# A decoder layer with experts: the router run by itself for the last two pairs, and new step orders and bank homes

## What is computed

```python
x = layernorm(x + attn(x, x, x, sa_..., causal=True))            # 16 heads of width 8
x = layernorm(x + attn(x, ctx, ctx, ca_..., causal=False))
rw = softmax(x @ router_w + router_b); topw, topi = top_k(rw, 2); topw = softmax(topw)
h = gelu(einsum('td,edf->etf', x, w1) + b1); eo = einsum('etf,efd->etd', h, w2) + b2
x = layernorm(x + sum over the two chosen experts of topw * eo)
```

## Time and profile before

| what | value |
|---|---|
| time, median of 3 runs | 417.77 us (416.07 to 417.9) |
| time of the profiled execution | 417.14 us |
| its span, first to last instruction | 415.4 us |
| busy: PE, PEld, DVE, ACT, POOL | 323.3, 240.7, 247.2, 224.1, 182.5 us |
| mean granted clock of PE | 0.889 of 2.4 GHz |

### The profile page before, as it was taken

How to read it: one execution, slowest core, us unless ns; L and a number is a source line. 1 busy time by engine, 2 the same in 40 slices (tenths; PEclk the granted TensorE clock), 3 DMA queues, 4 the chain that set the end, 5 groups by cost and what they waited for, 6 DMA issues and landing times. The chain is left out here.

```text
span 415.4 us, 8711 instructions
## 1 busy us (share of the span) xinstructions
PE 323.3 (78%) x2242; PEld 240.7 (58%) x2242; DVE 247.2 (60%) x793; ACT 224.1 (54%) x560; POOL 182.5 (44%) x260
## 2 busy tenths in 40 slices
PE   2589899998999889988798745886885779999400
PEld 1445576866767646655556422774684668999400
DVE  7062847585687772796564675254276554666356
ACT  4227385857867655666555512548653424556224
POOL 8404343451553583534834527002246556455422
PEclk9979999999999996999989965599798688999855
DMA  7453242344453532441437762322701123220053
GB/s 196 110 167 73 63 100 62 85 102 136 100 157 71 135 131 54 88 153 40 132 85 212 236 176 87 69 55 77 201 9 34 34 70 92 64 54 30 11 197 101
DMA packets 35047, 42.09 MB, mean 101 GB/s; under 512 B 5819, under 2 KB 26160, under 8 KB 35001
## 3 DMA queue, kind: packets, MB, share of 16 engines
q1 hardware_dynamic: 32728, 37.31, 33.8%
q0 software_dynamic: 2272, 4.24, 3.2%
HBM read 13.66 MB, written 14.79 MB: 68 GB/s over the span
## 5 line engine op out<-in xcount | busy, mean ns | idle before, releaser
L1426 POOL DMA_INDIRECT results<-sa_us,sa_pt x39 | 39.9, 1023 | 69.5 <-DVE sa_us L1326 65.7
L1056 ACT ACTIVATE sa_us<-bank,expert_b 128x128 f32<-128x128 f32 x156 | 44.7, 370 | 36.9 <-PE bank L905 36.3
L1391 POOL TENSOR_SCALAR_AFFINE_SELECT sa_pt<-sa_pt 128x512 f32<-128x512 f32 x64 | 38.7, 636 | 56.5 <-ACT sa_pt L1002 56.5
L1129 DVE TENSOR_REDUCE sa_nm<-bank 128x4 f32<-128x512 f32 x64 | 41.4, 685 | 20.9 <-PE bank L791 20.7
L918 PE MATMUL bank<-sa_over_qm,sa_us 128*128 x312 | 46.7, 298 | 8.4 <-ACT sa_us L1056 3.8
L918 PEld LDWEIGHTS bank<-sa_over_qm,sa_us 128*128 128x128 f32 x312 | 41.8, 208 | 11.8 <-issue 11.8
L905 PE MATMUL bank<-xsT,sa_pt 128*128 128x128 f32 x312 | 47.5, 301 | 1.3 <-DVE sa_pt L1314 1.0
L1002 ACT ACTIVATE ca_pt<-bank 77x512 f32<-77x512 f32 x64 | 34.4, 588 | 20.8 <-PE bank L811 20.8
L905 PEld LDWEIGHTS bank<-xsT,sa_pt 128*128 128x128 f32 x312 | 42.9, 212 | 3.3 <-DVE xsT L1313 1.5
L1421 POOL DMA_INDIRECT dispatched<-r_sent,r_row x32 | 31.1, 973 | 28.6 <-issue 17.1
L1129 DVE TENSOR_REDUCE ca_nm<-bank 128x4 f32<-128x308 f32 x64 | 27.6, 474 | 22.2 <-PE bank L791 21.8
(11 more groups left out here) (213 smaller groups left out, 752.2 us busy)
## 6 DMA issues: line engine op xcount, KB each, us to landing
dispatched<-filler SPq DMA_DIRECT2D x17, 520.0 KB, 4.7
sa_km<-sa_ku SPq DMA_DIRECT2D x32, 128.0 KB, 2.4
sa_qm<-sa_qu SPq DMA_DIRECT2D x32, 96.0 KB
ca_qm<-ca_qu SPq DMA_DIRECT2D x32, 96.0 KB
sa_pt<-dispatched SPq DMA_DIRECT2D x39, 65.0 KB, 1.8
ca_km<-ca_ku SPq DMA_DIRECT2D x32, 77.0 KB, 2.1
sa_over_km<-in_e_w SPq DMA_DIRECT2D x1, 2048.0 KB, 12.6
sa_pt<-results SPq DMA_DIRECT2D x8, 256.0 KB, 5.8
```

Source lines behind the costliest of these rows:

```text
L1056: act.activation(hid[n % 2][:, c, :], bank[b][:, P * (c if n < EARLY else c % 2):][:, 0:P], ACT.Gelu, bias=b1[:, bass.ds(expert * FC + c, ...
L1129: dve.tensor_reduce(k.nm[:, u, :, g], bank[home_of(p)[k, "scores", u][g % 2]][:, :].rearrange("q (j n) -> q j n", j=J)[:, :, 0:k.keys], AX ...
L1391: pool.affine_select(out=blockg, in_=blockg, compare_op=ALU.is_ge, fill=0.0, base=0, pattern=[[0, J], [1, P]], channel_multiplier=-1).then ...
L1426: pool.indirect_dma_start(out=results, out_offset=bass.IndirectOffsetOnAxis(ap=xs[n % RING][:, P:P + 1].bitcast(I32), axis=0), in_=ys[n % ...
```

## The change

For pairs 0 to 5 the router works as before. For pairs 6 and 7 it runs once for each pair, on that pair's two token tiles: 31 DVE operations instead of 33 (one running sum in place of three), each on half the columns; two exponentials on ACT for each pair; PE's `place` for each; and four transfers of POOL for each instead of eight for both. `routed_at` and `router_run` hold the counts that the waits use.

The fill of `dispatched` counts on two semaphores instead of one, so POOL waits for two values where it waited for one; the semaphore `s_fill` is gone and the filler counts on `s_pool_ones`.

All tables of `ORDER`, `FINAL`, `home` and `last_home` are new: the same steps in another order on each engine and in other banks.

```diff
-        ROUTER_OPS = 33
-        SELECTED = 20
+        ALONE = PAIRS - 2
+        def routed_at(p):
+            if p < ALONE:
+                return p % 2 == 1, slice(0, 4), p // 2 * 33, p // 2 * 33 + 20, p // 2 * 33 + 33
+            n = ALONE // 2 * 33 + (p - ALONE) * 31
+            return True, slice(2 * (p % 2), 2 * (p % 2) + 2), n, n + 18, n + 31
+        def router_run(p):
+            return p // 2 if p < ALONE else ALONE // 2 + p - ALONE
...
-                if p % 2 == 0:
+                runs, w, before, selected, after = routed_at(p)
+                if not runs:
                     return
...
-                pe.wait_ge(r.s_rt, n * ROUTER_OPS + SELECTED)
+                pe.wait_ge(r.s_rt, selected)
...
-                pool.wait_ge(s_filled, p * 32 + 32)
-                pool.wait_ge(r.s_rt, (p // 2 + 1) * ROUTER_OPS)
+                for n in range(p - (w.stop - w.start) // 2 + 1, p + 1):
+                    pool.wait_ge(s_filled[n % 2], n // 2 * 32 + 32)
+                pool.wait_ge(r.s_rt, after)
                 pool.wait_ge(r.s_xe1, p + 1)
-                for v in range(4):
+                for v in range(w.start, w.stop):
...
-            (CA, "mix", 0): (2,), (CA, "mix", 1): (5,), (CA, "norm", 0): (1,), (CA, "norm", 1): (4,),
+            (CA, "mix", 0): (1,), (CA, "mix", 1): (4,), (CA, "norm", 0): (1,), (CA, "norm", 1): (5,),
...
-            (CA, "weights", 1): (0, 3), (RT, "place", 0): (1,), (RT, "route", 0): (2, 2), (SA, "mix", 0): (2,),
+            (CA, "weights", 1): (7, 2), (RT, "place", 0): (4,), (RT, "route", 0): (2, 4), (SA, "mix", 0): (7,),
```

More of the change, by code:

```diff
@@ L306, in build @@
-            "pe": [
[L307 to L320, removed]
@@ new lines, in build @@
+                (CA, "weights", 1, 4), (RT, "gate", 0, 4), (SA, "project", 0, 7), (SA, "project_keys", 0, 7),
+                (MOE, "bias_columns", 0, 0), (SA, "turn_heads", 1, 5), (RT, "route", 0, 3), (SA, "shift", 0, 6),
+                (RT, "gate", 0, 3), (CA, "weights", 2, 4), (CA, "mix", 0, 4), (CA, "weights", 3, 4),
+                (SA, "weights", 0, 6), (SA, "weights", 1, 6), (CA, "turn", 0, 5), (RT, "second", 0, 3),
+                (SA, "shift", 1, 6), (CA, "spread_keys", 0, 5), (CA, "turn_context", 0, 6), (CA, "spread_keys", 1, 5),
@@ L484, in build @@
-                (CA, "project", 0, 6), (SA, "values", 0, 7), (CA, "norm", 1, 5), (SA, "restore", 0, 7),
-                (CA, "scores", 0, 6), (RT, "gate", 0, 5), (CA, "scores", 1, 6), (RT, "choose", 0, 5), (CA, "shift", 0, 6),
-                (RT, "second", 0, 5), (SA, "restore", 1, 7), (RT, "place", 0, 4), (RT, "place", 0, 5),
-                (RT, "number", 0, 5), (CA, "scores", 2, 6), (SA, "norm", 0, 7), (CA, "scores", 3, 6),
-                (CA, "project_keys", 0, 7), (CA, "shift", 1, 6), (MOE, "table", 0, 0), (RT, "second", 0, 6),
@@ L533, in build @@
-            (SA, "turn", 0): (2,), (SA, "turn_heads", 0): (3,), (SA, "turn_heads", 1): (6,), (SA, "values", 0): (0,),
-            (SA, "weights", 0): (4, 7), (SA, "weights", 1): (5, 6)}
+            (CA, "mix", 0): (4,), (CA, "mix", 1): (2,), (CA, "norm", 0): (4,), (CA, "project", 0): (1,),
+            (CA, "project_keys", 0): (5,), (CA, "restore", 1): (4,), (CA, "scores", 0): (5, 4), (CA, "scores", 1): (4, 5),
+            (CA, "shift", 0): (1,), (CA, "shift", 1): (5,), (CA, "spread_keys", 0): (0,), (CA, "spread_keys", 1): (3,),
@@ new lines, in build @@
+            (CA, "spread_terms", 1): (1,), (CA, "turn", 0): (4,), (CA, "turn_context", 0): (1,),
+            (CA, "turn_heads", 0): (5,), (CA, "turn_heads", 1): (5,), (CA, "values", 0): (5,), (CA, "weights", 0): (1, 2),
+            (CA, "weights", 1): (7, 5), (RT, "place", 0): (5,), (RT, "route", 0): (0, 7), (SA, "mix", 0): (1,),
+            (SA, "mix", 1): (0,), (SA, "norm", 0): (0,), (SA, "norm", 1): (4,), (SA, "project", 0): (1,),
+            (SA, "project_keys", 0): (0,), (SA, "restore", 1): (2,), (SA, "scores", 0): (4, 5), (SA, "scores", 1): (1, 6),
@@ L536, in home_of @@
+            (SA, "shift", 0): (0,), (SA, "shift", 1): (7,), (SA, "spread_terms", 0): (6,), (SA, "spread_terms", 1): (7,),
+            (SA, "turn", 0): (4,), (SA, "turn_heads", 0): (4,), (SA, "turn_heads", 1): (1,), (SA, "values", 0): (5,),
+            (SA, "weights", 0): (7, 0), (SA, "weights", 1): (3, 5)}
         def home_of(p):
@@ L1257, in _ @@
+                assert done[0] == after, done[0]
             tables = [0]
```

521 lines of the change are left out of this document (264 added, 257 removed).

## The result

The changed kernel takes 394.21 us (median of 4 runs, 391.07 to 396.04) against 416.92 for the kernel before on the same chip (4 runs, 415.55 to 417.9): a ratio of 0.945, 95% interval 0.938 to 0.952. That is 22.7 us faster, where 5.2 were forecast and the range ended at 402.5. The profiled execution, the longest of the four, has a span of 394.1 us and a time of 396.04. Medians are of all runs, ratios and intervals of the fast ones alone, and the profiles of three experiments (two table loads taken out, SP's list both ways) are of slow runs.

The account below looks back on a forecast made before the run. PE was taken as the bound, except at two places where a router's chain (DVE, then POOL's transfers) sets the end. Terms -0.9 + 0 - 2.7 + 2.5 - 4.1 = -5.2 took 417.14 to 411.9 us; range 402.5 to 421.

Parts of the forecast that it names:

- The sign: Whole kernel: the change makes it faster, by 5.2 us, from 417.14 to 411.9 us.
- Term 5: From `route` 7 to late tiles: four last-dispatch transfers instead of eight, first late `hidden` 25.2 us behind logits; -4.1 us.
- Term 3: Pair 5's router: less PE and DVE work ahead of it, so it comes earlier; -2.7 us.
- Term 1: Start: `spread_keys` goes ahead of four `spread_terms` matmuls, so the wait for the `sa_km` transfer shrinks; -0.9 us.
- Term 4: From `CA turn` 7 to `route` 7: gain ahead of `restore` 0, loss behind it; +2.5 us, bounds -3.2 to +5.7.
- Together -3.2: `CA turn` 7 to `restore` 0: work -2.9, longest wait -2.4, new wait of 2.1 ahead of `weights`; -3.2 us.
- +5.7: `restore` 0 to logits of pair 7: pair 6's router now stands inside, 19.8 us instead of 14.1.
- Term 2: Rotation, 30 to 225 us: same steps in another order and banks; 0 us, bounds -9.2 to +8.7.
- The clock did stay up: Rival, 260 to 314 us: PE at clock 1.00 instead of 0.86, 6.3 us less, 405.6 us; chance 0.18.
- The bank of `place`: Slower rival: next writer of bank 4 waits at two rotation places, 4.4 us each; 420.6 us, chance 0.18.
- Dearer switches: Rival: two ACT table switches after `gate` 7 cost twice their load, 2.6 us more; 414.5 us, chance 0.04.
- No change: Rival: no gain ahead of `restore` 0, pair 6's router costs all 5.7; 415.1 to 417 us, chance 0.19.

Follow-up runs that it names:

- `project` first: Kernel before with `project` ahead of `project_keys` on PE, ACT and DVE: 418.52 us, ratio 1.005 (1.001 to 1.008).

## Why the prediction was wrong

**The sign and two places were right.** Term 5 (-4.1) measured -4.4, and for its reason: the last dispatch began 12.7 us behind the logits, as forecast, and DVE's output of tile 16 came 23.1 us behind them, where 23.5 were forecast. The four transfers less are worth 5.2 us when put back, and the scatter of tile 8 was the last wait, 2.0 us of DVE's time. That the loads of the late tiles stand 0.8 us behind it, I had not seen. Term 3 measured about -2.8, if the 1.8 us of moved PE work are taken as given, beside 1.0 between logits and turn. Term 1 was mis-sized: the first scores came 2.2 us earlier, not 0.9, and 2.4 counted from PE's first matmul. The four matmuls of `spread_terms` give 0.85 of it, as forecast; I had taken the two waits ahead of the keys, 1.09 and 0.77 us, as fixed, and in the changed kernel one of 0.44 is left. `project` first does not do that alone.

**Term 4 failed (+2.5; measured -5.8).** The step that failed is "Together -3.2": from the turn to `restore` the time fell by 13.4. I let one wait go and took the other lengths of the old stretch as they were, above all the 6.6 us from `shift` to `weights`, to which I added a wait of 2.1. In the changed kernel these stand 4.05 us apart, and `weights` waits for nothing:

```profile
263.67 0.27 PE L804 MATMUL bank<-cst,ca_nm 128*16 128x128 f32 x1
...
267.72 0.71 PE L817 MATMUL bank<-ca_qm,ca_ku 128*77 128x512 f32 x2
```

From the turn to this `weights` 23.1 us became 18.1, and from there to `restore` 17.7 became 9.3. The runs show several causes, one behind the other: the transfer of the keys behind nine tile loads on SP and the wait for tile 1's copies, 3.4 us together and nothing in time for the second alone; ACT's alternation of exponential and Gelu, 5.6 us in the new order, 1.8 once the first two are gone from the old one, and 1.1 before that; the work of the second sequence, 6.2 us out of this part (with the first one's exponentials together) and 9.8 into the next in the old order; and a share of the clock. The 3.4 and the 6.2 would make 9.6 of the 13.4 if they add, which no run tried; the rest stays open. What the trace of before shows as one wait of 2.44 us is only the one that ended last. SP's order I had costed "at nothing", and in this term not at all.

Behind `restore` I put +5.7 down to pair 6's router; +7.6 was measured, and with the routers joined the stretch is as long. So the figure came near by luck. `norm` 1 came 14.6 us behind `restore`, where 15.5 were forecast, but from there to the logits it took 7.2 us and not the 4.3 of before.

**Term 2 failed (0; measured about -5).** From the first scores to pair 5's logits it was -6.8, of which -1.8 belong to term 3. PE's idle time between them fell from 21.2 to 17.8 us. The bounds (-9.2 to +8.7) held it, but my reason for 0, that no row spoke for either end, was the lack of a reading, not a finding. The two runs with SP's lists exchanged show how much stands there: 17 and 21 us in their profiles. Which of the many small waits gave the 5 us was not tried one by one. It stays open.

**The rivals.** The clock did stay up, as that rival said: from the turn to `restore` it was 0.95 instead of 0.81. What that is worth is shown in part only. Behind the wait of 2.44 us a full clock gave 1.0 to 1.5 us in the old order. The dip right behind the turn (0.56 up to the next `mix`) was not filled there, and at 0.50 the same work took 1.1 us longer. So some of the 13.4 us is the clock's, and how much stays open. The bank of `place` cost a `mix` of the rotation one wait of 0.6 us for the first operation of `number`, and decided nothing; the 2.2 us ahead of one `place` are put down to DVE's router (L1252), not to a bank. Dearer switches: no row has them. "No change" rested on the chain from turn to `weights` being fixed; it became 5.0 us shorter.

The range ended at 402.5 because each term's own bound was counted alone. With term 2 and the lower bound of term 4 together it would have reached 411.9 - 9.2 - 5.7 = 397.0, and still not 394: the bound of term 4 itself was wrong.

## What to carry to other kernels

A wait in a trace names what came last there, not what the place costs: here two edits that removed 1.6 and 2.4 us of visible waits gave nothing alone, and together with an earlier place in SP's queue 4 to 5 us. So price a reordered stretch by asking of every step which engine and which queue could deliver it earliest, SP's list of transfers included, instead of taking the old length minus the old waits. And an order of work is one thing over all engines: one engine's list from the other version cost 17 to 19 us either way.

## What was not expected of the hardware

In the changed kernel PE was idle for 6.6 of the 21.8 us from 277 to 298.8, in waits of at most 1.47 us, and the granted clock was 1.00 throughout. In the kernel before it fell to half behind one wait of 2.44 us, and was 0.71 from there to `restore`. Twenty small transposes in that wait kept it at 1.00. PE then was busy for 2.9 us less on that way, which became 1.5 us shorter: here busy time at half clock overstates what the clock costs, as PE also waits.
